# A gate Silu that waits for two of three banks, and h turned ahead of x, in the FFN tail of a two-layer language-model tower

## The reference, cut to what matters

```python
h = h + _L1_attn_ref(_layernorm(h), ...)      # ends in a recurrence over 128 steps:
#   state = silu(d_t + state) + p_t ;  out = states @ out_w.T + out_b
h = h + _L1_ffn_ref(_layernorm(h), w_gate, w_up, w_down)

def fp4_linear(x, w):                          # both rounded to FP4 in blocks of 16
    return einsum('bsk,nk->bsn', fp4_quant_dequant(x), fp4_quant_dequant(w))
gate = fp4_linear(x, w_gate)                   # 256 -> 704
y = fp4_linear(x, w_up)                        # 256 -> 704
h = silu(gate) * y
return fp4_linear(h, w_down)                   # 704 -> 256
```

## Time and profile before

| | |
|---|---|
| median of 3 runs | 634.71 us (633.86 to 637.6) |
| the profiled execution | 637.28 us, its span 635.3 us |
| PE busy | 547.1 us (86%) |
| DVE busy | 454.4 us (72%) |
| ACT busy | 252.2 us (40%) |
| POOL busy | 215.3 us (34%) |
| mean granted TensorE clock | 0.945 |

### The profile page before, as it was taken

The page is one execution under the profiler, slowest core; times in us unless marked ns, Lnnn a source line. Parts: engine busy times, 40 slices in busy tenths (PEclk is TensorE's granted clock), DMA queues, the critical chain, the costliest instruction groups (busy, mean ns, idle before and its releaser), DMA issues.

```text
span 635.3 us, 9416 instructions
## 1 busy us (share of the span) xinstructions
PE 547.1 (86%) x3062; PEld 331.1 (52%) x3062; DVE 454.4 (72%) x1120; ACT 252.2 (40%) x781; POOL 215.3 (34%) x412
## 2 busy tenths in 40 slices
PE   2888969999998998998998998993569998989884
PEld 2665445555555555655645644741235555555553
DVE  1254757778778788788787786486678898988852
ACT  1263026326326326316416515802335444443321
POOL 6406561222213213114114113021347767664110
PEclk9879889999999999999999998996579999999997
DMA  6800100000000000000000000003300000000000
GB/s 189 248 2 27 34 25 1 2 0 0 0 0 0 0 0 0 0 0 0 0 0 0 0 0 2 1 2 68 64 1 10 17 8 18 9 18 17 9 17 17
DMA packets 13517, 12.75 MB, mean 20 GB/s; under 512 B 2795, under 2 KB 12724, under 8 KB 13492
## 3 DMA queue, kind: packets, MB, share of 16 engines
q1 hardware_dynamic: 12212, 10.34, 6.1%
q0 software_dynamic: 1280, 2.11, 1.2%
HBM read 8.25 MB, written 2.10 MB: 16 GB/s over the span
## 4 chain that ended last, share of the span: by engine, by line
PE 54%; DVE 12%; issue 10%; ACT 9%; POOL 8%; SPq 4%; DMA 2%; DVEq 0%; POOLq 0%; ACTq 0%
PE psum L657 13%; PE psum L919 8%; PE psum L941 5%; ACT probs L999 4%; PE psum L597 4%; SPq L383 3%; PE psum L739 3%; PE psum L575 2%; POOL rstd L428 2%; PE psum L601 2%; PE psum L750 2%; PE psum L719 2%; DVE stats L1292 2%; POOL rstd L425 2%; PE psum L732 1%
## 5 line engine op out<-in xcount | busy, mean ns | idle before, releaser
L657 PE MATMUL psum<-expw_sb,n2T 128*128 128x512 f32 x256 | 119.1, 609 | 0.0
L425 POOL TENSOR_TENSOR rstd<-meanvar,ln_eps_col 128x1 f32<-128x1 f32 x64 | 17.8, 278 | 288.2 <-DVE meanvar L1296 288.1
L919 PE MATMUL psum<-wguT,n2T 128*128 128x512 f32 (+1 forms) x192 | 82.8, 583 | 0.0
L999 ACT ACTIVATE probs<-psum,neg_max 128x128 f32<-128x128 f32 x256 | 69.1, 391 | 33.4 <-DVE neg_max L1315 33.3
L657 PEld LDWEIGHTS psum<-expw_sb,n2T 128*128 128x128 f32 x256 | 47.2, 194 | 47.6 <-issue 47.6
L941 PE MATMUL psum<-wdT,probsT 128*128 128x256 f32 x192 | 50.3, 405 | 12.7 <-ACT probsT L967 12.7
L919 PEld LDWEIGHTS psum<-wguT,n2T 128*128 128x128 f32 x192 | 38.1, 200 | 39.5 <-issue 34.4
L1315 DVE TENSOR_REDUCE neg_max<-psum 128x4 f32<-128x512 f32 x64 | 40.4, 681 | 19.7 <-PE psum L601 19.7
L967 ACT ACTIVATE probsT<-psum 128x512 f32<-128x512 f32 x72 | 37.2, 530 | 30.6 <-PE psum L611 26.0
L1143 ACT ACTIVATE probs<-u_now 64x16 f32<-64x16 f32 x128 | 27.4, 214 | 53.9 <-POOL u_now L517 37.9
L941 PEld LDWEIGHTS psum<-wdT,probsT 128*128 128x128 f32 x192 | 35.2, 196 | 25.8 <-issue 21.0
(11 more groups left out here) (172 smaller groups left out, 1025.7 us busy)
## 6 DMA issues: line engine op xcount, KB each, us to landing
expw_sb<-in_expert_w SPq DMA_DIRECT2D x8, 256.0 KB
expw_sb<-hidden SPq DMA_DIRECT2D x16, 128.0 KB
result<-res SPq DMA_DIRECT2D x16, 128.0 KB
w_raw<-in_w_down SPq DMA_DIRECT2D x1, 704.0 KB, 9.4
w_raw<-in_w_gate SPq DMA_DIRECT2D x1, 640.0 KB, 7.1
w_raw<-in_w_up SPq DMA_DIRECT2D x1, 640.0 KB, 8.2
wexp_sb<-in_w_expand SPq DMA_DIRECT2D x1, 256.0 KB, 3.1
wproj_sb<-in_w_project SPq DMA_DIRECT2D x1, 256.0 KB, 3.2
```

The lines of the kernel that those rows point to most:

```text
L657: last = mm(pq[:, g, :], n2T[:, u, k, :], expw_sb[:, k, EPQ * g:EPQ * (g + 1), :].rearrange("p e n -> p (e n)"), start=(k == 0), stop=(k = ...
L919: last = mm(pgu[u][:, c0:c1], xqT[:, u, k, :], wguT[:, k, c0:c1], start=(k == 0), stop=(k == KD - 1))
L999: last = nc.scalar.activation(probs[:, u, h, :], pq[:, g, j * T:(j + 1) * T], ACT.Exp, bias=neg_max[:, u, h:h + 1])
```

## The change

`gate_up` raises a new semaphore, `gate_part`, when the product of its second bank is done; `silu` waits for that instead of the whole product, and `h_product`, which reads the third bank too, waits for the whole product as well as for Silu. On PE and on ACT, the turning of h (tile j) goes ahead of that of x (tile j+2). The pair of semaphores `conv_last` becomes one that counts to eight.

```diff
--- before.py
+++ after.py
@@ -255,7 +255,7 @@
         mix_step = sems("mix_step", 2)
         h3_done = sem("h3_done")
         xn3T_done, n3T_ready = sem("xn3T_done"), sem("n3T_ready")
-        conv_dve, conv_pool, conv_last = sem("conv_dve"), sem("conv_pool"), sems("conv_last", KD)
+        conv_dve, conv_pool, conv_last = sem("conv_dve"), sem("conv_pool"), sem("conv_last")
         in_done, p_stored, dt_ready = sem("in_done"), sem("p_stored"), sem("dt_ready")
         rank_done, delta_done, d_stored = sem("rank_done"), sem("delta_done"), sem("d_stored")
 
@@ -266,7 +266,8 @@
         st_ready, outp_done, h4_done = sem("st_ready"), sem("outp_done"), sem("h4_done")
         qx = sems("qx", 9)
         xqT_done, xqT_ready = sem("xqT_done"), sem("xqT_ready")
-        gu_done, sil_gate, hm_ready = sem("gu_done"), sem("sil_gate"), sem("hm_ready")
+        gate_part, gu_done = sem("gate_part"), sem("gu_done")
+        sil_gate, hm_ready = sem("sil_gate"), sem("hm_ready")
         qh = sems("qh", 9)
         hqT_done, hqT_ready = sems("hqT_done", 2), sems("hqT_ready", 2)
         down_done, res_ready = sem("down_done"), sem("res_ready")
@@ -884,7 +885,7 @@
                     values(1)
                 if last_pair:
                     of_rank(1)
-                    project_in(1, conv_last, (TAPS, TAPS))
+                    project_in(1, (conv_last, conv_last), (TAPS, 2 * TAPS))
                     delta(1, 2, 0, pfront[1])
 
 
@@ -918,6 +919,9 @@
                     for k in range(KD):
                         last = mm(pgu[u][:, c0:c1], xqT[:, u, k, :], wguT[:, k, c0:c1],
                                   start=(k == 0), stop=(k == KD - 1))
+                    if c == 1:
+
+                        last.then_inc(gate_part, 1)
                 last.then_inc(gu_done, 1)
 
             def h_transposed(j):
@@ -955,9 +959,9 @@
                     outp(j + 4)
                 if j + 1 < TILES:
                     gate_up(j + 1)
+                h_transposed(j)
                 if j + 2 < TILES:
                     x_transposed(j + 2)
-                h_transposed(j)
                 down(j)
 
 
@@ -1158,7 +1162,7 @@
 
             def silu(j):
                 u = j % 2
-                act.wait_ge(gu_done, j + 1)
+                act.wait_ge(gate_part, j + 1)
                 wait(act, hm_ready, j - 1)
                 nc.scalar.activation(sil[:, u, :], pgu[u][:, 0:INNER], ACT.Silu).then_inc(sil_gate, 1)
 
@@ -1529,8 +1533,8 @@
                     if last_pair:
                         projected(0, 1, 0)
                         deltas(0, 1, 0, pfront[0])
-                        convolved(0, 1, 2, 0, conv_last[0], 0)
-                        convolved(1, 1, 2, 0, conv_last[1], 0)
+                        convolved(0, 1, 2, 0, conv_last, 0)
+                        convolved(1, 1, 2, 0, conv_last, TAPS)
                         projected(1, 2, 0)
                         deltas(1, 2, 0, pfront[1])
                 if front:
@@ -1579,6 +1583,7 @@
 
             def h_product(j):
                 u = j % 2
+                dve.wait_ge(gu_done, j + 1)
                 dve.wait_ge(sil_gate, j + 1)
                 wait(dve, qh[8], j - 1)
                 V.tensor_tensor(hm[:, u, :], sil[:, u, :], pgu[u][:, INNER:2 * INNER],
```

## The result

The changed kernel takes 628.22 us (median of 20 runs, 621.87 to 633.8), the kernel before 633.66 (20 runs, 629.27 to 637.89). The two medians are 5.4 us apart. The ratio leaves out three runs of the changed kernel (631.44 to 633.8) that are over 1.5% above its fastest: it is 0.9887, with a 95% interval of 0.9857 to 0.9917, or 7.2 us less, between 5.3 and 9.1. The forecast was 627.0 us, 7.7 less, 1.2%.

A forecast was written before the change was run, and what follows sets the result against it. A tile was taken as bound by TensorE's work plus a round trip to ScalarE. 14 x 0.50 = 7.0 us and 0.73 at the end, sum 7.7, from a median of 634.7 gave 627.0 us; range 624.4 to 631.8.

The forecast's parts named there:

- TensorE's loop: Per tile, TensorE's work plus a round trip to ScalarE; period to go from 10.08 to 9.58 us, gain 0.50.
- Fourteen times 0.50: Down products 0 to 13, each ahead of a later gate and up product, gain 0.50 us each, 7.0 in all.
- the store of 0.4 us: Rescaled h due at -0.18, ready at about -0.6, so 0.4 us can be lost before TensorE sees anything.
- the other loop: The loop of VectorE, POOL and ScalarE, forecast at 9.53 us per tile, under TensorE's 9.58.
- The cover: Whether the VectorE, POOL and ScalarE loop stays under TensorE's: forecast 9.53 us against 9.58, by a hair.
- The wait at the sizes: VectorE's fp4 chain reaches the step needing ScalarE's sizes too early, at +5.03, and goes on at +5.45: 0.42 us lost.
- The end: Last tile: h_product(15) goes at +0.08 instead of +0.81, its chain to the last store being the path: 0.73 us more.
- rival F: Last six transposes and down product: if TensorE's clock held after the shorter idle, some 2.5 us more, 624.5; chance 0.07.
- B: One more collision: VectorE's multiply for x beats a POOL step, loop 9.8, 1.9 us lost, time 628.9; chance 0.20.
- C: More collisions of POOL steps with VectorE, loop 10.1, nothing gained in the ten tiles, time 631.6; chance 0.08.
- D: The second bank's flag comes only with the whole product, so only the swap works: 3.6 us, time 631.1; chance 0.05.
- E: Slower: h_product and the reduction lock out POOL's x rescaling and states, loop 10.6, time 637.3; chance 0.05.

The follow-up runs named there:

- e3: Changed kernel with the turned h copied in three pieces of two blocks, down product started after the first; 621.69 us, ratio 0.9817, later 623.35 us.
- e4: Changed kernel with one small POOL operation added per tile right before the rescaling of h; 625.58 us in one run.
- e8: Changed kernel with POOL's fifth recurrence step of a tile made to wait for VectorE's multiply of x; 629.36 us in one run.
- e5: On top of e3, the sizes of h taken on ScalarE after four recurrence steps instead of five; 626.71 us in one run.
- e1: Only the first half of the change: Silu let go by the second bank, x still turned ahead of h; 626.03 us, ratio 0.9906 against the kernel before.
- c1: The changed kernel as it is, run again on one chip with e3's kernel; 627.36 us, ratio 0.9902 against the kernel before.

## Why the prediction was right

The mechanism is the one forecast, and one term, the fourteen periods, was put too high.

**TensorE's loop.** The 0.50 us per tile is 0.49 in twelve tiles. Down at +1.21 for +1.19, Silu at -1.26 for -1.28, the end of Silu's wait, the 0.26 of the x copy: all as worked out. Each half alone was forecast at 9.80 and 9.82 and gave 9.81 and 9.83.

**Fourteen times 0.50.** The first two of the fourteen gave 0.35 and 0.14: 9.67 and 9.94 where 10.02 and 10.08 had been. In the second trace of the changed kernel they gave 0.08 and 0.15. That is the term that was mis-sized, 7.0 against 6.35 measured. I had counted the store of 0.4 us from the tile I read and not from the first one. The trace of before shows it: in the tile at 486.50 POOL's rescaling ends 0.29 ahead of the product's end, in the next 0.36, and only from 506.65 on the 0.8 that I used; the swap asks for 0.18. The stage begins with the other loop late. In the changed kernel's second tile POOL's third step meets the big multiply and takes 0.89, and the rescaled h comes 0.3 late (transposes at 484.08, when they were due at 483.78). The first row is of before, the others of the changed kernel:

```profile
484.82 1.39 POOL L498 TENSOR_TENSOR hq<-wgu_tmp,hsc 128x704 f32<-128x704 f32 x1
...
477.62 0.89 POOL L518 TENSOR_TENSOR u_now<-probs,drive 64x16 f32<-64x16 f32 x1 [0.33 <-ACT probs L1147]
...
482.64 1.39 POOL L499 TENSOR_TENSOR hq<-wgu_tmp,hsc 128x704 f32<-128x704 f32 x1
...
484.08 0.87 PE L932 MATMUL psum<-ident,hq 128*128 128x128 f32 x6
```

**The cover.** "Loop 9.53, under 9.58 by a hair": e3 measures 9.57, and e4 and e8 show that what is added there comes out in the period. The wait at the sizes was put at 0.42 and is 0.34. Since 9.57 and 9.59 are 0.02 apart and the stage starts late, the store comes back slowly: rescaled h is ready 0.16 ahead of the transposes in the tile shown (503.16, 503.32), not 0.4, and some 0.03 more in each tile after it, until it is 0.38 (568.70 + 1.39 against 570.47). h_product, forecast within 0.1 of the product's end, is at +0.33 in the tile shown. It stands behind VectorE's last fp4 steps for x. The first of them runs into POOL's rescaling and ends 0.28 us behind it (502.01 + 1.43, against 501.77 + 1.39; it takes 0.41 in e5, where it runs ahead of the rescaling), and so h_product is late when the rescaling is; with the store it comes back, to +0.12, and it is at +0.03 in the tiles without recurrence. That sign failed for most tiles and cost TensorE nothing there, since the transposes still start on time:

```profile
568.70 1.39 POOL L499 TENSOR_TENSOR hq<-wgu_tmp,hsc 128x704 f32<-128x704 f32 x1 [1.13 <-DVE wgu_tmp L1258]
...
570.47 0.82 PE L932 MATMUL psum<-ident,hq 128*128 128x128 f32 x6
```

**The end.** 0.73 was forecast and 0.66 came; the last down product took 5.05 us for 4.94. TensorE idles 3.63 us for 4.21, the transposes still take 1.54 us for all six, at a granted clock of 0.50, 1.2 GHz: rival F did not happen.

**The merged conv_last.** It was put at nothing, and the traces agree: the changed kernel's lead is 2.22 us near 407 us, ahead of the last pair's convolution (427 to 438 us), and 2.19 at the second product's end, behind it.

**The other rivals.** B: the race was won by POOL in every tile with recurrence, by 0.02 to 0.03. C did not happen. D is out by the row at 502.23. E is out by the two POOL rows inside h_product and the reduction (0.62 and 0.45, as before).

The absolute time, 627.0 for 628.2, is nearer than it deserves, by luck: the median of the kernel before was 634.7 in three runs and is 633.7 in twenty. From 633.7 my gain of 7.7 makes 626.0, which is 2.2 off.

## What to carry to other kernels

A wait for the last part of a product can often be one for the part that is read, and it pays only with what stands behind it in the reader's queue: here about half of the gain was the order of two copies. Before shortening a loop, add up the next one with the waits that the shortening itself moves; here it had 0.02 us less, and the next 0.43 us taken from TensorE gave nothing in the tiles that had both. Look at the first tiles too: a store read in the steady part may not be there at the start.

## What the runs showed of the hardware

The four traces compared here reach the second product's end up to 8.5 us apart, ahead of the changed stage. The same VectorE instructions start at (us):

| | before | changed | e1 | changed again (c1) |
|---|---|---|---|---|
| a reduction into `g_small` | 119.58 | 117.30 | 111.93 | 116.34 |
| mean and variance of a layer norm | 383.15 | 380.92 | 375.44 | 379.86 |
| an addition to `hidden` | 407.26 | 405.04 | 399.38 | 408.08 |
| end of the second gate and up product | 476.48 | 474.29 | 468.54 | 477.08 |

Between the first two rows the differences stay within 0.1 us. So they arise ahead of 120 us, but for c1, which loses 4.1 us between the second row and the third. The windows (busy us and counts of PE, PEld, DVE, ACT and POOL, granted clock of TensorE, DMA share, GB/s) differ in where the clock is low. Of before and the changed kernel again:

```profile
25.00:50.00 25.00, 22.38 (x163) 17.26 (x163) 9.76 (x20) 14.14 (x47) 4.53 (x6) 0.80 0.13 45
...
380.00:405.00 25.00, 21.90 (x188) 13.97 (x188) 15.96 (x30) 15.53 (x48) 6.22 (x9) 0.93 0.01 2
```

```profile
25.00:50.00 25.00, 21.44 (x196) 15.61 (x196) 11.66 (x27) 15.39 (x50) 6.08 (x10) 1.00 0.11 36
...
380.00:405.00 25.00, 22.16 (x155) 14.32 (x155) 13.31 (x23) 14.26 (x45) 6.23 (x9) 0.73 0.01 2
```

Between 130 and 380 us all four have 1.00. c1's loss lies where it has 0.73 (380 to 405 us) and the other three 0.93. Ahead of 120 us, before and the changed kernel have 0.80 and 0.81 in the stretch from 25 to 50 us, e1 and c1 have 1.00, and e1 also has 0.94 from 50 to 80 us where the others have 0.89; e1 is 7.7 us ahead of before there and c1 3.2. The stretches are cut by time and not by work, so the price of one of them can't be read off; before and the changed kernel have nearly the same values up to 80 us, before has the higher one from 80 to 105 us (0.86, 0.80), and yet before is the later by 2.3 us. What sets a low stretch off was not tried.

The POOL step that meets VectorE's big multiply ends just behind it, whenever it started: 0.08 us after it in the changed kernel (507.21 + 0.52 against 506.76 + 0.89), 0.09 where it started 0.09 behind the multiply and took 0.89 (477.62). The Trainium skill, page "SBUF — State Buffer", section "Who interferes with whom", has an exclusive lock there that the earlier one holds; the rows at 507.21 and 508.06 agree with it.
